# Scattering a_dst during the projection, and PSUM operands in the attention tile

## What is computed

```
h = (x_flat @ W_gat).reshape(M, HEADS, NUM_EXPERTS)          # M = 32768, 4 heads, 4 experts
a_src = (h * att_src).sum(-1);  a_dst = (h * att_dst).sum(-1)
e = leaky_relu(a_src[src] + a_dst[dst], 0.2)
e_max = segment_max(e, dst);  ee = exp(e - e_max[dst])
denom = segment_sum(ee, dst)
agg = segment_sum(h[src] * (ee / denom[dst])[:, :, None], dst)
scores = layernorm(agg + b_gat).mean over heads;  gates = softmax over the top 2 of 4 experts
```

## Time and profile before

| | us |
|---|---|
| median of three runs | 20784.96 |
| the profiled execution | 20795.29 |
| its span, first to last instruction | 20793.7 |
| POOL busy | 10284.8 |
| DVE busy | 7812.9 |
| PE busy | 6756.5 |
| ACT busy | 3617.8 |

### The profile page before, as it was taken

One profiled execution on the slowest core, in us unless ns is written; L12 is line 12 of the kernel. 1 busy time (PEld: TensorE's weight loads), 2 busy tenths in 40 slices (PEclk: granted clock), 3 DMA queues, 4 the chain that ended last, 5 costly groups with the idle time before them and its releaser, 6 DMA issues. The chain is left out here.

```text
span 20793.7 us, 223509 instructions
## 1 busy us (share of the span) xinstructions
PE 6756.5 (32%) x79070; PEld 3146.8 (15%) x79070; DVE 7812.9 (38%) x10937; ACT 3617.8 (17%) x6239; POOL 10284.8 (49%) x10259
## 2 busy tenths in 40 slices
PE   0277711000000000059789999740000000000079
PEld 0122301000000000024245555320000000000034
DVE  9866589111111111244478888510111111111244
ACT  0122201000000000023655555620000000000023
POOL 0011278777777777742100000147777777777710
PEclk8588855555555555579899999965555555555589
DMA  1000211221111111136311111521111112211145
GB/s 40 18 30 30 63 35 23 43 42 41 41 39 39 39 39 39 35 82 143 83 51 45 45 45 43 162 78 29 39 39 39 39 39 42 43 39 39 27 100 130
DMA packets 787024, 1072.74 MB, mean 52 GB/s; under 512 B 287476, under 2 KB 503636, under 8 KB 765652
## 3 DMA queue, kind: packets, MB, share of 16 engines
q1 hardware_dynamic: 405844, 612.28, 10.4%
q0 software_dynamic: 343104, 219.83, 7.6%
q10 hardware_dynamic: 37440, 230.74, 3.1%
HBM read 671.93 MB, written 390.08 MB: 51 GB/s over the span
## 5 line engine op out<-in xcount | busy, mean ns | idle before, releaser
L894 POOL DMA_INDIRECT g_got<-table,g_ring x8192 | 8280.6, 1011 | 2496.9 <-issue 2496.9
L1118 PE MATMUL g_rowsP<-g_eye,g_meta 128*20 128x128 f32 x12 | 2.9, 416 | 10765.2 <-DVEq L1162 10765.2
L1010 DVE TENSOR_TENSOR g_z<-g_gs,g_pr 128x512 f32<-128x512 f32 x64 | 44.7, 699 | 8725.5 <-DMA g_gs<-rows 8725.5
L980 ACT ACTIVATE g_out<-g_u 128x512 f32<-128x512 f32 x64 | 40.3, 630 | 10747.0 <-DVE g_d L1025 10747.0
L1118 PEld LDWEIGHTS g_rowsP<-g_eye,g_meta 128*20 128x20 f32 x12 | 1.5, 142 | 10765.9 <-DVEq L1162 10765.4
L2070 POOL DMA_DIRECT2D m_x<-x x64 | 34.4, 537 | 2507.2 <-POOLq L1539 2500.8
L1359 PE MATMUL f_hP<-f_xn,f_w 128*128 128x512 f32 x2048 | 967.1, 595 | 699.4 <-DMA f_xn<-xn 699.4
L1366 PE MATMUL f_oP<-f_hid,f_w 128*128 128x512 f32 x2048 | 962.1, 592 | 0.0
L1388 ACT ACTIVATE f_hid<-f_hP,f_b 128x512 f32<-128x512 f32 x1024 | 647.5, 683 | 1122.3 <-PE f_hP L1359 1122.3
L526 POOL DMA_INDIRECT cb_got<-dst,k_blki x256 | 248.8, 972 | 1141.1 <-DVE cb_le L537 1078.1
L962 POOL DMA_INDIRECT ad<-g_nodes,k_start_row x512 | 695.6, 1359 | 182.3 <-issue 155.4
(11 more groups left out here) (402 smaller groups left out, 16200.3 us busy)
## 6 DMA issues: line engine op xcount, KB each, us to landing
g_got<-table,g_ring POOLq DMA_INDIRECT x8192
f_gate<-gates SPq DMA_DIRECT2D x128, 1024.0 KB
rows<-g_got SPq DMA_DIRECT2D x512, 192.0 KB, 1.9
g_gs<-rows ACTq DMA_DIRECT2D x64, 1536.0 KB, 6.3
state<-g_out ACTq DMA_DIRECT2D x64, 1536.0 KB, 6.0
h_x<-x SPq DMA_DIRECT2D x128, 256.0 KB
xn<-h_xn POOLq DMA_DIRECT2D x128, 256.0 KB
f_xn<-xn SPq DMA_DIRECT2D x128, 256.0 KB, 3.5
```

The costliest lines, as they stand in the source:

```text
L894: pool.indirect_dma_start(self.got[:,par,k,:],None,self.table,bass.IndirectOffsetOnAxis(ap=self.ring[:,par,k:k+1].bitcast(u32),axis=0)).th ...
```

## The change

The 256 scatters of a_dst move from the head of the attention stage into the projection, four to a tile, from `hs`. There partition p of group q of tile i holds node (4i+q)*128+p, so `start_row` is turned to that order: two transposes on PE and two strided copies at the end of `Bounds`. The two stores of the projection's tile move from POOL's queue to ACT's, the waits for their landing to SP's. In the attention stage POOL's queue begins with the fetch of first rows and the gathers, SP loads the edges first, and waits for nodes and identity at its end. In the attention tile `cont`, `brk`, the spread a_dst and the maxima (`adm`), the scaled score and the decay (`low`) and a second copy of the weights (`wP`) are in PSUM; ACT scales the score and copies the maxima to `out`. To make room in PSUM, the counts and the side sums of `Ordering` and `Bounds` use parts of other tiles. The diff, without the declarations and renamings that the text above covers:

```
+        self.ident=r.sb("ident",[P,P])
+        self.edgeP=r.pb("edge",[P,3,P])
+        self.sideP=self.edgeP[:,2,0:1]
...
-        do(V.tensor_tensor(keep.start_row[:,:],self.tmp[:,:],self.start[:,:],ALU.add))
+        do(V.tensor_tensor(self.tmp[:,:],self.tmp[:,:],self.start[:,:],ALU.add))
+        dve.sem_inc(self.ended,1)
+        dve.wait_ge(self.moved,2)
+        for v in range(2): V.tensor_copy(keep.start_row[:,:].rearrange("p (a v) -> p v a",v=2)[:,v,:],self.edgeP[:,v,:])
     def tensor_end(self,pe):
+
+
+        pe.wait_ge(self.ended,2)
+        for v in range(2): last=self.nc.tensor.transpose(self.edgeP[:,v,:],self.tmp[:,v*P:(v+1)*P],self.ident[:,:])
+        last.then_inc(self.moved,1)
...
+            bounds.tensor_shift(pe)
             bounds.tensor_end(pe)
...
-            paired(sp,TILES,load)
+            xn_stores.start(sp)
+            t_stores.start(sp)
+            def stored(i,par):
+                xn_stores.landed(sp,i,par)
+                t_stores.landed(sp,i,par)
+            for i in range(4):
+                load(i,i%2)
+                if i==3: stored(0,0)
+            with sp.Fori(2,TILES//2) as t:
+                for par in range(2):
+                    load(t*2+par,par)
+                    stored(t*2+par-3,1-par)
+            for i in range(TILES-3,TILES): stored(i,i%2)
...
                 t_stores.done.before(act,i,2)
+                sent_done.before(act,i,2)
                 nc.scalar.copy(hs[:,par,:,:],hp[par][:,:,:]).then_inc(copied.sem,1)
+                nc.scalar.dma_start(xn_out[:,bass.ds(i*T,T)],xn[:,par,:]).then_inc(xn_stores.sems[par],16)
+                copied.of(act,i)
+                nc.scalar.dma_start(table[bass.ds(i*T,T),:].rearrange("(q p) f -> p q f",p=P),hs[:,par,:,:]).then_inc(t_stores.sems[par],16)
             lagged(act,TILES,[lambda i,par: nm.act_square(act,i,par),lambda i,par: nm.act_root(act,i,par),body])
         @block.gpsimd
         def _(pool):
-            def body(i,par):
-                nm.normed.of(pool,i)
-                pool.dma_start(xn_out[:,bass.ds(i*T,T)],xn[:,par,:]).then_inc(xn_stores.sems[par],16)
+            sent_done.start(pool)
+            def landed_rows(i):
+                pool.wait_ge(sent[i%2],(i//2+1)*64)
+                pool.sem_inc(sent_done.sem,1)
+            for i in range(TILES):
                 copied.of(pool,i)
-                pool.dma_start(table[bass.ds(i*T,T),:].rearrange("(q p) f -> p q f",p=P),hs[:,par,:,:]).then_inc(t_stores.sems[par],16)
-                xn_stores.landed(pool,i,par)
-                t_stores.landed(pool,i,par)
-            xn_stores.start(pool)
-            t_stores.start(pool)
-            paired(pool,TILES,body)
+                pool.sem_inc(send_gate,1)
+                for q in range(4):
+                    k=i*4+q
+                    pool.indirect_dma_start(ad,bass.IndirectOffsetOnAxis(ap=keep.start_row[:,k:k+1],axis=0),hs[:,i%2,q,20:24],None).then_inc(sent[i%2],16)
+                if i: landed_rows(i-1)
+            landed_rows(TILES-1)
...
+            prc=r.sb("prc",[P,2,4])
             z=r.sb("z",[P,C,4])
             u=r.sb("u",[P,C,4])
             d=r.sb("d",[P,C,4])
-            dd=r.sb("dd",[P,C,4])
+            seam=r.pb("seam",[P,2,C])
+            cont,brk=seam[:,0,:],seam[:,1,:]
+            adm=r.pb("adm",[P,C,4])
+            low=r.pb("low",[P,C,4])
+            wP=r.pb("wP",[P,C,4])
             out=r.sb("out",[P,2,C+1,HW])
...
+                if order: order.sync(sp)
                 sp.dma_start(nodes[:,:,:],table.rearrange("(p n) f -> p n f",p=P)).then_inc(n_in,16)
                 sp.dma_start(ident[:,:],eye).then_inc(n_in,16)
-                if order: order.sync(sp)
                 g.sync(sp)
+                sp.wait_ge(n_in,32)
             @block.gpsimd
             def _(pool):
                 if order: order.pool(pool)
-                pool.wait_ge(n_in,32)
-                pool.sem_inc(send_gate,1)
-                for i in range(HI//SEND):
-                    par=i%2
-                    if i>=2:
-                        pool.wait_ge(sent[par],(i-par)//2*SEND*16)
-                        pool.sem_inc(send_gate,1)
-                    for k in range(i*SEND,(i+1)*SEND):
-                        pool.indirect_dma_start(ad,bass.IndirectOffsetOnAxis(ap=keep.start_row[:,k:k+1],axis=0),nodes[:,k,20:24],None).then_inc(sent[par],16)
                 pool.indirect_dma_start(rowfirst[:,:],None,table,bass.IndirectOffsetOnAxis(ap=keep.first[:,:],axis=0)).then_inc(first_in,16)
                 g.pool(pool)
...
-                weighed.start(act)
-                for s in sent: act.wait_ge(s,HI//2*16)
+                for f in (scaled,kept,weighed): f.start(act)
...
+                    shaped.of(act,i)
+                    nc.scalar.activation(low[:,:,:],z[:,:,:],ACT.Copy,scale=0.2).then_inc(scaled.sem,1)
+                    topped.of(act,i)
+                    if not (isinstance(i,int) and i==0): nc.scalar.copy(out[:,par,0,20:24],out[:,1-par,C,20:24])
+                    nc.scalar.copy(out[:,par,1:C+1,20:24],adm[:,:,:]).then_inc(kept.sem,1)
                     shifted.of(act,i)
+                    nc.scalar.activation(wP[:,:,:],u[:,:,:],ACT.Exp)
                     nc.scalar.activation(out[:,par,1:C+1,16:20],u[:,:,:],ACT.Exp)
-                    nc.scalar.activation(dd[:,:,:],d[:,:,:],ACT.Exp).then_inc(weighed.sem,1)
+                    nc.scalar.activation(low[:,:,:],d[:,:,:],ACT.Exp).then_inc(weighed.sem,1)
...
-                    V.tensor_tensor(cont[:,:],ds[:,par,1:C+1],ds[:,par,0:C],ALU.is_equal).then_inc(same.sem,1)
+                    V.tensor_tensor(cont,ds[:,par,1:C+1],ds[:,par,0:C],ALU.is_equal).then_inc(same.sem,1)
                     same.of(dve,i)
-                    V.tensor_scalar(brk[:,:],cont[:,:],-1.0,FAR,ALU.add,ALU.mult).then_inc(broken.sem,1)
+                    V.tensor_scalar(brk,cont,-1.0,FAR,ALU.add,ALU.mult).then_inc(broken.sem,1)
                     landed(dve,e_in,i,par)
                     if begin:
                         dve.wait_ge(first_in,16)
                         V.tensor_copy(ed[:,0,0,:],rowfirst[:,20:24]).then_inc(began,1)
                         dve.wait_ge(began,2)
                     for h in range(4):
-                        ins=V.tensor_tensor_scan(pr[:,par,:,h],cont[:,:],ed[:,par,:,h],0.0 if begin else pr[:,1-par,C-1,h:h+1],ALU.mult,ALU.add)
+                        ins=V.tensor_tensor_scan(adm[:,:,h],cont,ed[:,par,:,h],0.0 if begin else prc[:,1-par,h:h+1],ALU.mult,ALU.add)
                     ins.then_inc(known.sem,1)
                     known.of(dve,i)
+                    V.tensor_copy(prc[:,par,:],adm[:,C-1,:])
                     landed(dve,g_in,i,par)
-                    V.tensor_tensor(z[:,:,:],gs[:,par,:,16:20],pr[:,par,:,:],ALU.add).then_inc(shaped.sem,1)
-                    shaped.of(dve,i)
-                    V.scalar_tensor_tensor(z[:,:,:],z[:,:,:],0.2,z[:,:,:],ALU.mult,ALU.max).then_inc(leaky.sem,1)
+                    V.tensor_tensor(z[:,:,:],gs[:,par,:,16:20],adm[:,:,:],ALU.add).then_inc(shaped.sem,1)
+                    scaled.of(dve,i)
+                    V.tensor_tensor(z[:,:,:],z[:,:,:],low[:,:,:],ALU.max).then_inc(leaky.sem,1)
                     leaky.of(dve,i)
                     broken.of(dve,i)
                     if not early: dve.wait_ge(out_in[par],(i-par)*8)
                     if begin: V.memset(out[:,0,0,20:24],-FAR)
-                    else: V.tensor_copy(out[:,par,0,20:24],out[:,1-par,C,20:24])
                     for h in range(4):
-                        ins=V.tensor_tensor_scan(out[:,par,1:C+1,20+h],brk[:,:],z[:,:,h],-FAR if begin else out[:,1-par,C,20+h:21+h],ALU.add,ALU.max)
+                        ins=V.tensor_tensor_scan(adm[:,:,h],brk,z[:,:,h],-FAR if begin else out[:,1-par,C,20+h:21+h],ALU.add,ALU.max)
                     ins.then_inc(topped.sem,1)
                     topped.of(dve,i)
-                    V.tensor_tensor(d[:,:,:],out[:,par,0:C,20:24],out[:,par,1:C+1,20:24],ALU.subtract).then_inc(fallen.sem,1)
-                    V.tensor_tensor(u[:,:,:],z[:,:,:],out[:,par,1:C+1,20:24],ALU.subtract)
+                    kept.of(dve,i)
+                    V.tensor_tensor(u[:,:,:],z[:,:,:],adm[:,:,:],ALU.subtract)
+                    V.tensor_tensor(d[:,:,:],out[:,par,0:C,20:24],adm[:,:,:],ALU.subtract).then_inc(fallen.sem,1)
                     fallen.of(dve,i)
-                    V.tensor_tensor(d[:,:,:],d[:,:,:],brk[:,:].unsqueeze(2).broadcast_to([P,C,4]),ALU.add).then_inc(shifted.sem,1)
+                    V.tensor_tensor(d[:,:,:],d[:,:,:],brk.unsqueeze(2).broadcast_to([P,C,4]),ALU.add).then_inc(shifted.sem,1)
                     weighed.of(dve,i)
-                    V.tensor_tensor(out[:,par,1:C+1,0:16].rearrange("p c (h e) -> p c h e",e=4),gs[:,par,:,0:16].rearrange("p c (h e) -> p c h e",e=4),out[:,par,1:C+1,16:20].unsqueeze(3).broadcast_to([P,C,4,4]),ALU.mult).then_inc(spread.sem,1)
```

(38 more changed lines are left out.)

14 lines of the change are left out of this document (4 added, 10 removed).

## The result

Four runs of the changed kernel took 19,794 to 19,842 us, median 19,821.5; the kernel before took 20,786.4 beside them (20,767 to 20,813). The ratio is 0.9534 [0.9517, 0.9552]: faster by 965 us. The profiled execution is the slowest of the four: 19,842.5 us, span 19,840.9.

The account below looks back on a forecast made before the run. POOL was taken to bound both attention stages (scatters, then gathers) and the projections; 20,795 - 326 - 322 - 436 + 198 + 9 = 19,918 us. Its own range, 19,840 to 20,010 us, was widened to 19,835 to 20,270 us for rivals.

Parts of the forecast that it names:

- (1): Second attention stage: with the scatters gone, gathers start earlier; 326 us gained.
- (2): First attention stage: with the scatters gone, gathers start earlier but beside the sort, at 62% progress; 322 us gained.
- (3): Attention tiles: gathers no longer held by DVE instructions with two SBUF inputs; 436 us gained.
- (5): Ends of involution and first experts stage, last tile of each attention stage: small added work, 9 us lost.
- A: Attention tiles: the twenty scans go on holding gathers; gain 106 rather than 436 us, time 20,248 us; chance 0.13.
- B: Projections: SP's interleaving or ACT's queue becomes the bound, some 9 us a tile; time 20,283 us; chance 0.09.
- D: Attention stages: gathers start no earlier or run no faster despite the scatters' removal; time 20,566 us; chance 0.02.
- C: Projections: landing of 16-byte rows becomes the bound, slower than before; 21,051 us at 15 us a tile; chance 0.02.
- (4): Projections: four added scatters a tile raise the period from 4.60 to 6.15 us; 198 us lost in all.

Follow-up runs that it names:

- after_again: The changed kernel run once more, unchanged, as base for the follow-up runs; 19,834 us, ratio 0.9540.
- land_now: Against the changed kernel, POOL waits in each projection tile for that tile's own scatters to land, not the previous tile's; 20,024 us, ratio 0.9634.
- four_hs: Against the changed kernel, four hs buffers instead of two, so ACT's copy waits for landings four tiles back; 19,823 us, ratio 0.9537.
- lag_four: Against the changed kernel, SP waits between its loads for the stores of tile j-4, not j-3; 19,811 us, ratio 0.9526.

## Why the prediction was wrong in its number and right in its other parts

(1) Held. The first gather of the second stage came 12.2 us after the stage's start (13413.47 after 13401.29), and 338.3 us after it before: 326 us gained, 326 predicted. Its own mark was 18 us; the loads landed in 10.

(2) Held. The first gather of the first stage came at 21 us (2761.38 after 2739.99) and no longer at 538, and those beside the sort made 61% progress where 62% was taken.

(3) Held: the busy time went down by 223.5 us for all gathers, though 510 of them now stand beside the sort and some 260 did before. After it they take 0.9455 us each (3,364.96/3,559 in 3720 to 8170 us). The longest gather of 8.21 us is at 2764.83, beside the sort and not in a tile. In the second stage 4,095 periods took 5,121.6 us where 5,329.3 before: −208 of −218. The missing 10 us are 3 ns more per gather in that trace; in after_again, with the old 944 ns, the stage is 10.2 us shorter.

(5) Held. The two casts of the turned first rows end at 2372.36, 1.3 us after the DVE addition that was the last step before (2371.02); 1.5 was predicted. From the last gather's start to the last store of states it is 30.1 us (18535.05 to 18565.19) against 28.6 before, +1.5 where 3 was said: three more ACT operations, but faster scans (8.77 against 9.02 us).

Rivals A, B and D are refuted by the tile's timeline, by 5.4 to 5.6 us a tile, and by the first gathers. C's landing never became the bound: POOL's own waits for landed rows were 4.6 us in all in the first projection and 2.1 us in the second. The kernel after gives no landing times for its scatters, but land_now does, and its scatters run beside the same loads and stores. Its first projection has:

```profile
DMA to landing us min/median/max: 2.1/2.1/3.4
```

C also rested on a misread row. The 31.4 us in the earlier trace rows are a landing of the 16 stores that clear `ad` in the program's first 30 us (15.7 to 31.4 us). The scatters beside the 7 MB of loads landed in 2.1 to 9.4 us, median 3.1.

(4) is the step that failed, in its size: "Period 6.01 us; with 0.14 us ... 6.15 us. Against 4.60 us: 1.55 x 64 = 99 us a projection, 198 us in all". Measured were 5.38 and 5.63 us, +55 and +79 us, 134 in all; after_again has +48 and +70, 118. The step laid report, copy and POOL's reaction of 0.80 us one behind the other after the last scatter, and the runs show that they are hidden behind scatters already queued. The 0.80 us came from a row in which POOL had been idle for 7.49 us, and a sequencer that has nothing queued is another case than one that is three scatters ahead. land_now made the serial chain real, with the landing in it: the next scatter came 2.04 us after the last had ended and 0.51 us after the copy, so even an idle POOL reacted faster there than in the earlier trace rows. The 0.1 us each for report and ACT's wake had no row. four_hs made the wait looser and found nothing to gain, and in lag_four the copy waits for the report 58 times while the tile takes 5.24 us. The lower bound that the step named, "5.10 us a tile if the copy overlaps", was the right case. Over it stood SP's loads, called "just hidden" and in truth late 42 times by up to 4.2 us; against lag_four's 5.24 us a tile they cost 0.14 and 0.39 us in this trace, 34 us in all; in after_again the two projections lost 19 us to them.

The account closes against the profiled execution: −953 us measured, −877 predicted, 76 more. Of these (4) gave 64. Mamba and the involution gave 30: over the 13 traces they took 3,507 to 3,565 and 1,396 to 1,420 us with nothing in them changed but the ends. The attention stages gave back 17 (−529 and −532 where −537 and −541 were due), mostly the 3 ns a gather. With (4) at its measured 118 to 134 us the sum is 19,838 to 19,854 us, inside the range, and so is the profiled execution. But the sum starts from an execution 10 us over the median before, so against the medians it is 19,828 to 19,844 us: (4) alone takes the forecast to the low end of the range. The last 14 us are then spread from run to run (Mamba alone moves by more), for which the range had no term; on which side of 19,835 the median fell was chance.

The range was also too narrow for its own terms. Downward they are 62 us (2), 8 us (3, up to the bound of 444) and 77 us (4); combined as independent errors that is about 100 us, so 19,820 us and not 19,840. And 77 us for (4) is less than the 134 us between the step's value and its own lower bound.

## What to carry to other kernels

A wait and a semaphore increment between indirect DMAs on POOL cost nothing while DMAs are queued before them; price the hand-off to another engine only where POOL would stand idle, as land_now did. Where DVE and a gathering POOL overlap, put one of DVE's two tensors in PSUM, above all for a chain of scans with a pointer initial value. When a cost has a case at which it vanishes, the range has to reach that case.

## What the runs showed of the hardware that was not expected

- POOL's sequencer was three scatters ahead of its engine. With scatters queued the gap before the next was the ordinary 0.30 us; where POOL was idle, the next scatter started 0.51 us after the copy (2567.79 to 2568.30) and 2.04 us after the last scatter's end.
- A gather of POOL (0.94 us undisturbed) was held by DVE instructions with two SBUF inputs: 2.56 us beside the multiply, 5.95 and 6.39 us beside scans with a pointer, 1.24 us beside scans with a constant. Beside scans with one input in PSUM it took 0.95 us, with a pointer or a constant.
- The same gathers have a median of 944 ns in some runs and 947 in others of one kernel, 10 us an attention stage. Two traces should be compared only with this in mind.
- A scatter of 16-byte rows lands in 2.1 us (median) beside almost nothing, and in 2.1 us, at most 3.4, beside the loads and stores of land_now's first projection.
